# Deformable block: the loads of y are issued by the sync engine, between its loads of the hats, instead of by ScalarE

## The reference, cut to what matters

```
# block 0
y   = conv1x1(relu(bn(conv3x3(relu(bn(conv1x1(x)))))))         # 1024 -> 256 -> 256 -> 1024
x1  = relu(x + softplus(residual_scale) * bn(y))
# block 1
a   = relu(group_norm(conv1x1(x1)))                            # 1024 -> 256
om  = conv3x3(a) + b_off                                       # 27 channels: 9 x-, 9 y-offsets, 9 masks
s   = bilinear_sample(a, grid + offsets) * sigmoid(mask)       # 9 taps, 14 x 14 pixels, 256 channels
b   = relu(group_norm(einsum('bckhw,ock->bohw', s, w2)))
out = relu(group_norm(conv1x1(b)) + x1)                        # 256 -> 1024
```

## Time and profile before

| | us |
|---|---|
| median of three runs | 3158.97 (3150.49 to 3162.46) |
| the profiled execution | 3153.34 |
| span of its trace | 3151.6 |
| TensorE (matmul) busy | 2998.2 (95%) |
| VectorE busy | 2310.0 (73%) |
| ScalarE busy | 1807.0 (57%) |
| GpSimd busy | 738.7 (23%) |

### The profile page before, as it was taken

The page is one execution under the profiler, slowest core; times in us unless marked ns, Lnnn a source line. Parts: engine busy times, 40 slices in busy tenths (PEclk is TensorE's granted clock), DMA queues, the critical chain, the costliest instruction groups (busy, mean ns, idle before and its releaser), DMA issues.

```text
span 3151.6 us, 47048 instructions
## 1 busy us (share of the span) xinstructions
PE 2998.2 (95%) x16864; PEld 2936.3 (93%) x16864; DVE 2310.0 (73%) x4756; ACT 1807.0 (57%) x3313; POOL 738.7 (23%) x455
## 2 busy tenths in 40 slices
PE   8998999998998499999999999999999999999996
PEld 8998999998998399999999999999999999999996
DVE  4655555544565468888888888888888888888885
ACT  4444222224665356666666766776667666766664
POOL 0000000000000133333333333333333333333331
PEclk9999999999999599999999999999999999999998
DMA  6553000002554334444444444444444444444431
GB/s 227 185 189 115 1 1 1 1 1 103 208 211 177 123 120 152 140 144 154 154 140 147 149 152 144 148 155 141 153 149 154 139 155 151 150 141 154 151 114 72
DMA packets 190681, 414.89 MB, mean 132 GB/s; under 512 B 17552, under 2 KB 160880, under 8 KB 185584
## 3 DMA queue, kind: packets, MB, share of 16 engines
q1 hardware_dynamic: 144368, 309.11, 28.6%
q10 hardware_dynamic: 46080, 102.78, 10.2%
HBM read 296.42 MB, written 115.40 MB: 131 GB/s over the span
## 4 chain that ended last, share of the span: by engine, by line
PE 51%; DVE 14%; ACT 1%; DMA 1%; issue 0%; POOL 0%; SPq 0%; ACTq 0%; POOLq 0%; DVEq 0%
PE work L69 6%; PE work L71 6%; PE work L70 6%; PE sample L69 6%; PE deform L69 5%; PE sample L70 5%; PE sample L71 5%; PE deform L70 5%; PE deform L71 5%; DVE x L1279 3%; DVE x L1166 3%; DVE s_lo L1261 2%; DVE x_lo L1172 2%; DVE v_lo L1269 2%; DVE aT_lo L1252 1%; PE work L1416 1%
## 5 line engine op out<-in xcount | busy, mean ns | idle before, releaser
L1127 POOL TENSOR_TENSOR hats<-hats 98x784 f32<-98x784 f32 (+1 forms) x320 | 625.9, 1956 | 821.9 <-DMA hats<-hat_scratch 787.0
L989 ACT ACTIVATE v_hi<-sample 128x392 fp32r<-128x392 f32 (+1 forms) x640 | 295.8, 462 | 325.4 <-PE sample L71 303.9
L69 PE MATMUL sample<-s_hi,aT_hi 98*128 98x392 f32 (+1 forms) x1280 | 428.2, 335 | 21.2 <-DVE s_lo L1261 18.1
L69 PE MATMUL deform<-v_hi,w_w 128*128 128x392 f32 x1152 | 409.6, 356 | 15.4 <-DVE v_lo L1269 15.4
L70 PE MATMUL sample<-s_lo,aT_hi 98*128 98x392 f32 (+1 forms) x1280 | 421.5, 329 | 0.0
L71 PE MATMUL sample<-s_hi,aT_lo 98*128 98x392 f32 (+1 forms) x1280 | 420.3, 328 | 0.0
L70 PE MATMUL deform<-v_lo,w_w 128*128 128x392 f32 x1152 | 392.1, 340 | 0.0
L71 PE MATMUL deform<-v_hi,w_w 128*128 128x392 f32 x1152 | 391.8, 340 | 0.0
L1269 DVE TENSOR_TENSOR v_lo<-sample,v_hi 128x392 fp32r<-128x392 f32 (+1 forms) x640 | 326.3, 517 | 69.8 <-ACT v_hi L989 68.8
L1261 DVE TENSOR_TENSOR s_lo<-hats,s_hi 98x784 fp32r<-98x784 f32 (+1 forms) x320 | 332.8, 1040 | 11.6 <-ACT s_hi L980 10.1
L980 ACT ACTIVATE s_hi<-hats 98x784 fp32r<-98x784 f32 (+1 forms) x320 | 251.8, 787 | 115.2 <-DVE x L1166 77.0
(11 more groups left out here) (147 smaller groups left out, 7473.7 us busy)
## 6 DMA issues: line engine op xcount, KB each, us to landing
hats<-hat_scratch SPq DMA_DIRECT2D x768, 150.1 KB
x_in<-in_x SPq DMA_DIRECT2D x32, 1568.0 KB, 6.4
y_scratch<-y_out SPq DMA_DIRECT2D x32, 1568.0 KB, 5.1
x<-in_x SPq DMA_DIRECT2D x64, 784.0 KB, 6.2
y_in<-y_scratch ACTq DMA_DIRECT2D x256, 196.0 KB, 2.9
out<-x ACTq DMA_DIRECT2D x64, 784.0 KB, 3.4
hats<-hat_scratch SPq DMA_DIRECT2D x192, 75.0 KB
hat_scratch<-offs_b SPq DMA_DIRECT2D x128, 96.5 KB
```

Of the source, the lines that this page charges most:

```text
L69: nc.tensor.matmul(out, w_hi, x_hi, start=start, stop=False)
L989: nc.scalar.activation(v_hi[:, group % 2, c, 0:taps_of(g), i, :], sample[:, t % 2, 0:cols(g)].rearrange("p (k s) -> p k s", s=PIX), ACT.Co ...
L1127: nc.gpsimd.tensor_tensor(hats[:, slot, 0:2, 0:n], hats[:, slot, 0:2, 0:n], hats[:, slot, 2:3, 0:n].broadcast_to([HALF, 2, n]), ALU.mult). ...
```

## The change

`load_y` moves, with its waits, from ScalarE's program to SyncE's, and its eight calls get places in SyncE's list of steps. The loads of the last two weight arrays, `wo` and `w3`, which are issued once before the first pair, move up in the same list, to a place ahead of the first loads of y.

```
             def step(past, before, now, after, coming):          # SyncE
+                load_y(after, 5)
+                load_y(after, 6)
                 load_hats(now, 4)
                 load_hats(now, 5)
+                load_y(after, 7)
                 load_hats(now, 6)
                 load_hats(now, 7)
                 load_x(coming, 0)
                 load_hats(now, 8)
                 load_x(coming, 1)
+                if after is None and coming is not None:
+                    wo.load(sp, wo_stage, woff_source)
+                    w3.load(sp, w3_stage, w3_source)
                 store_hats(after, 1, 0)
                 store_hats(after, 1, 1)
                 store_hats(after, 0, 0)
                 store_hats(after, 0, 1)
                 load_hats(now, 9)
+                load_y(coming, 0)
+                load_y(coming, 1)
                 load_hats(after, 0)
+                load_y(coming, 2)
+                load_y(coming, 3)
                 load_hats(after, 1)
+                load_y(coming, 4)
                 load_hats(after, 2)
                 load_hats(after, 3)
-                if after is None and coming is not None:
-                    wo.load(sp, wo_stage, woff_source)
-                    w3.load(sp, w3_stage, w3_source)
...
             def step(past, before, now, after, coming):          # ScalarE
                 part_s(before, 7)
-                load_y(after, 1)
                 make_distance(now, 0)
...
                 part_v(before, 12)
-                load_y(after, 2)
                 part_s(before, 8)
...
                 make_x1(after, 1)
-                load_y(after, 3)
...
                 part_aT(now, 0)
-                load_y(after, 4)
...
                 rectify(past, 4)
-                load_y(after, 5)
...
                 part_v(now, 2)
-                load_y(after, 6)
                 rectify(past, 6)
                 part_v(now, 3)
-                load_y(after, 7)
                 rectify(past, 7)
...
                 part_v(now, 10)
-                load_y(coming, 0)
```

More of the change, by code:

```diff
@@ L844, in load_hats, with load_y @@
             @of_pair
+            def load_y(p, k):
+                if k == 0:
+                    at_least(sp, om_lo_made, p.n)
+                at_least(sp, plus_y, KX * p.n + k - 1)
+                sp.dma_start(y_in[:, k % 2].rearrange("p i s -> p (i s)"), y3[p.n][:, k, :]
+                              ).then_inc(y_loaded[k % 2], 16)
+            @of_pair
             def load_hats(p, u):
@@ L898, in store_out @@
                               ).then_inc(out_stored[p.buf][i], 16)
[L900 to L906, removed]
             @of_pair
```

## The result

The changed kernel takes 3417.55 us (median of six runs, 3413.24 to 3421.57), the kernel before beside it 3155.8 us (six runs, 3150.49 to 3163.06). The ratio is 1.0824, with a 95% interval of 1.0805 to 1.0843: 262 us more. The prediction had 3390 us, in a range of 3280 to 3485.

A forecast was written before the change was run, and what follows sets the result against it. TensorE was taken to bound the kernel, busy 297.04 of 300 us. 4.6 + 2.0 + 1.2 = 7.8 us a pair, times 30, is 234 us; on 3153.34 that is 3387, stated as 3390, range 3280 to 3485.

The forecast's parts named there:

- The chain: Chunk 0's load, behind SyncE's stores and unit 9's loads, delays VectorE 6.33 us and stops TensorE at `sample_tile` 15 every pair.
- Chunk 0 with its clock: At `sample_tile` 15: a TensorE stop of 4.6 us plus 2.0 us for a lowered clock, in 30 pairs.
- The split into a stop and a clock: At `sample_tile` 15: stop 6.33 - 1.73 = 4.6 us; clock fall 2.6 us in three pairs of four, 2.0 a pair.
- TensorE's slack of 1.73 us: Time from the end of VectorE's `rest_v` 13 to the start of `sample_tile` 15 before the change, subtracted from 6.33 us.
- two waits of VectorE: VectorE standing for late y before `add_y` 0, 6.33 us, and before `add_y` 7, about 1.6 us, each pair.
- Chunk 7, 1.2 us: Its load behind unit 5 of the hats makes the sum 1.6 us late; less 0.40 slack, TensorE stops 1.2 us before `conv1`.
- The sum: Loss per pair 4.6 + 2.0 + 1.2 = 7.8 us, times 30 is 234 us.
- Chunks 2 and 3, costed at nothing: Their loads wait for sums that are late themselves and land before VectorE comes to them; no cost.
- The relief of ScalarE at nothing: Eight issues and a 2.65 us wait leave ScalarE, 5.3 us a pair; covered by TensorE's backlog, so no gain.
- The signs I had named: Expected in the profile after: longer period, VectorE idle before `add_y`, TensorE idle before samples and `conv1`, granted clock below 1.00.

The follow-up runs named there:

- e6: Kernel before, with only the loads of chunks 0 and 1 of y moved to their places in SyncE's list; 3344.09 us, 1.0585.
- e1: Changed kernel, with the loads of chunks 0 and 1 of y moved ahead of the four stores of hats; 3253.44 us, 1.0301.
- e4: Kernel before, with chunks 0, 1 and 2 of y issued later in ScalarE's own list, SyncE's queue untouched; 3329.86 us, 1.0538.
- e9: Changed kernel, with 24 unused products of 128x392 in TensorE's list before `sample_tile` 15; 3403.24 us, 1.0774.
- e2: Changed kernel, with the load of chunk 7 of y moved ahead of unit 5 of the hats; 3351.61 us, 1.0613.
- e3: Changed kernel, with chunks 0 and 1 of y ahead of the stores of hats and chunk 7 ahead of unit 5 of the hats; 3198.15 us, 1.0125.
- e7: Changed kernel, with chunks 0 and 1 ahead of the stores, 7 ahead of hats unit 5, 2 and 3 ahead of the next pair's unit 0; 3169.47 us, 1.0028.
- e8: Kernel before, with the load of chunk 2 of y moved behind `part_s` 8 and `part_v` 13 in ScalarE's own list; 3160.75 us, 1.0007.
- e5: Changed kernel, with 64 unused products of 128x96 in TensorE's list before `sample_tile` 15; 3545.3 us, 1.1226.
- e10: Changed kernel, with 32 unused products of 128x96 in TensorE's list before `sample_tile` 15; 3421.83 us, 1.0853.

## Why the prediction was right, and where it wasn't

- **The chain.** Right. A load that was out early now stands behind stores that wait for ScalarE's hats, its sum makes VectorE late, and TensorE pays once a pair. e6 shows it with this place alone, e1 by taking it away, and e4 that a late issue does it from ScalarE's queue too, so it isn't SyncE's queue as such.
- **Chunk 0 with its clock, 4.6 + 2.0 us for 30 pairs, 198 us.** Measured as 185 us where it is added alone (e6), 166 where it is taken out of the whole (e1), and there chunk 2 begins to cost. The stop was forecast as 4.6 and is 4.79 us in the pair shown, by errors that cancel. From the issue at 2218.91 to the sum at 2221.62 is 2.71 us, where I took 3.9. But the issue came 6.30 us after the first store instead of 5.56 (the four stores took 3.83 us, not 3.21), and the three `add_x1` behind the sum took 2.84 instead of 2.08 us; GpSimd's product of hats ran at the same time (1.18 of the 2 us from 2222), and I haven't tested whether that is the cause.
- **The split into a stop and a clock.** Wrong in kind, though the sum came near. I took TensorE's slack of 1.73 us off VectorE's 6.33 and added 2.0 for the clock. The ledger has 2.4 for the clock, but e9 gives only 0.5 us back with the clock held (at most 1.1). As I read it, the slack isn't saved, since VectorE is now the late engine of the following stretch, and TensorE meets it again at the next waits. VectorE's whole wait is about what a pair loses, and a low clock beneath it is mostly hidden. The prediction's own two waits of VectorE, 6.33 + 1.61 = 7.94 us (7.85 measured), taken in full for 31 pairs, give 246 us. That the engine is 0.86 busy in the steady stretch should have told me that it can't make up 6 us at once.
- **Chunk 7, 1.2 us.** Mis-sized: 68 us by e2, 55 by e3 against e1, 2.2 and 1.8 us a pair. In the pair shown VectorE waits 2.23 us for it, where I had 1.6, and again nothing of it is slack: TensorE's two stops at `conv1` are 0.53 + 0.83 = 1.36 us, near my 1.2.
- **The sum.** Partly luck. 234 us were forecast and 262 measured, but chunk 0 was taken 13 to 32 us too high (198 against 185 and 166) and chunk 7 19 to 32 us too low (36 against 55 and 68), and these errors offset each other.
- **Chunks 2 and 3, costed at nothing.** Wrong once the sum of chunk 0 is on time: 31 us, between e3 and e7. I had argued that they wait for late sums anyway. In the changed kernel that cover holds, since the wait list has 45 waits of VectorE in 20.7 pairs, and by its timeline 41 of them are for chunks 0 and 7 and none for chunk 2 or 3. It is a cost that appears only when the greater ones go.
- **The relief of ScalarE at nothing.** Right in the time, by e8 (1.0007) for the wait and by e7 for wait and issues together. The reason given was TensorE's backlog; the trace of e8 adds that ScalarE waits for TensorE at the same place, so most of the relief never reaches it.
- **The signs I had named.** A period of 72 us (71.8; but it was built on one pair of 64.5, and the mean of before is 63.4, so the sum of 7.8 would have made 71.2), TensorE waiting 4 to 5 us a pair for v_lo (4.7), a gap before `conv1` of about 1 (1.6), the clock near 0.97 (0.95 over 1500 to 3000 us), VectorE 6 us idle in front of `add_y` (7.85, two places together).

The rule of the Trainium skill that I set against the forecast, page "DMA: Bandwidth & Descriptors", section "Issuing engines are not separate DMA queues", says that the queues of all issuers share the same DMA engines. The runs agree as far as it goes: y lands in 2.9 us from SyncE's queue (e3) and in 3.0 from ScalarE's, and with all issues at good places the time is within 0.3% of before (e7). The 262 us come from what the sentence doesn't cover, the place of an issue in a list that waits.

The places don't simply add. In the change chunk 2 is covered, so what is to be compared with its 262 us is 185 + 68 = 253; the 31 us of chunks 2 and 3 appear only once chunk 0 is in time, and then belong to the 96 of e1 and the 41 of e3. What stays open: the 10 us of e7, the slower `add_x1` beside GpSimd, and the part of e9's 2.4 us that no wait accounts for.

## What to carry to other kernels

Before a DMA is moved to another engine's list, look up the time at which it was issued and the time at which its new neighbour ahead was released: the difference is its delay. Here the bandwidth of the queues hardly mattered beside it. Follow that delay to the engine that waits for the data, and if this engine has little slack over a whole period, count its wait in full, without the slack that the bounding engine has at the next hand-over; that came closer in every version here. Undoing the largest of several such places can uncover the next, so look for them together. And before a wait is called a cost, look whether another stands right behind it, as ScalarE's did in e8.

## What the runs showed of the hardware

- Narrow products did not hold the clock. In the pair shown, 64 products of 128x96 took 10.03 us, and the clock was 0.61 and then 0.50 in stretches in which TensorE's row was busy all the time (e5). 32 of them took 3.67 us, and the clock was at its lower level for 5.0 us a pair instead of 7.2 (e10). 24 products of 128x392 took 4.42 us at the same place, and the mean clock from 1500 to 3000 us was 1.00, with 0.7 us a pair at the lower level (e9). e9 and e10 differ in the length of the filler as well as in the width.
- The clock can fall behind stops that are each under 1 us. In e3 TensorE stopped for 0.96 and then for 0.92 us, and the clock went to 0.50 (columns as in the earlier trace rows):

```profile
2137.61 0.44 PE L69 MATMUL deform<-v_hi,w_w 128*128 128x392 f32 x1 [0.96 <-DVE v_lo L1269]
...
2139.87 0.69 PE L69 MATMUL sample<-s_hi,aT_hi 98*128 98x392 f32 x1 [0.92 <-DVE s_lo L1261]
```

```profile
2136.00:2140.00 4.00, 2.13 (x11) 1.47 (x9) 4.00 (x6) 2.48 (x6) 1.86 (x1) 0.99 0.66 237
2140.00:2144.00 4.00, 4.00 (x13) 4.00 (x14) 2.90 (x11) 1.75 (x3) 0.00 (x0) 0.50 0.37 115
```
